# A bf16 copy of every second weight matrix, made once in HBM during the scan stage and read back by the MLP stages

## The reference, cut to what matters

```python
# layer 0, x is (4, 4096, 1024) f32
a = layernorm(x)
a2 = a + ssm_scan(rmsnorm(a, scale1), A, B, C, D)          # 16 states for each of 1024 channels
x = x + a2 + gelu(rmsnorm(a2, scale2) @ w1 + b1) @ w2 + b2  # w1 1024x4096, w2 4096x1024
u = layernorm(x)
x = x + u + sum over 2 shared experts of gelu(xn @ W1_s + b1_s) @ W2_s + b2_s
          + sum over the 2 chosen of 8 routed experts, weighted, of gelu(xn @ W1_r + b1_r) @ W2_r + b2_r
```

## Time and profile before

| what | us |
|---|---|
| median of 3 runs | 8356.27 |
| the runs | 8684.81, 8317.97, 8356.27 |
| the profiled execution | 8311.05 |
| its span, slowest core (core 2) | 8309.1 |
| spans of the 8 cores | 8291.6 to 8309.1 |
| PE busy, DVE busy, ACT busy, POOL busy | 5283.8, 2353.1, 1454.8, 1666.5 |

### The profile page before, as it was taken

One profiled execution on the slowest core, in us unless ns is written; L12 is line 12 of the kernel. 1 busy time (PEld: TensorE's weight loads), 2 busy tenths in 40 slices (PEclk: granted clock), 3 DMA queues, 4 the chain that ended last, 5 costly groups with the idle time before them and its releaser, 6 DMA issues.

```text
span 8309.1 us, 62744 instructions; the slowest of 8 cores (8291.6 to 8309.1 us)
## 1 busy us (share of the span) xinstructions
PE 5283.8 (64%) x22583; PEld 2288.5 (28%) x23040; DVE 2353.1 (28%) x2813; ACT 1454.8 (18%) x2046; POOL 1666.5 (20%) x1608
## 2 busy tenths in 40 slices
PE   0000000000787268889888898888888899888997
PEld 0000000000332123333333343333333334333333
DVE  5889898989112510000000000000000000000001
ACT  4760000000211021112111221112211122111220
POOL 0009696946000000001100111000110001001010
PEclk9855555555898689999999999999999999999997
DMA  3100000000453046666667666676666666666664
GB/s 92 23 0 0 5 0 5 0 5 3 62 84 56 15 76 99 104 102 91 99 104 106 91 96 92 102 106 87 96 92 103 100 95 92 95 102 102 91 92 105
DMA packets 555731, 597.23 MB, mean 72 GB/s; under 512 B 13194, under 2 KB 366362, under 8 KB 553764
## 3 DMA queue, kind: packets, MB, share of 16 engines
q0 software_dynamic: 545280, 566.28, 46.4%
q1 hardware_dynamic: 7844, 18.54, 0.7%
q10 hardware_dynamic: 2304, 8.39, 0.2%
HBM read 1134.22 MB, written 12.58 MB: 138 GB/s over the span
## 4 chain that ended last, share of the span: by engine, by line
PE 49%; DMA 19%; issue 14%; DVE 11%; POOL 5%; ACT 1%; DVEq 0%; POOLq 0%; ACTq 0%; SPq 0%
PE ps L873 23%; PE ps L907 18%; DMA WBUF<-W2r 11%; POOL SSb L266 4%; DMA STAT<-W1r 3%; PE ps L691 3%; DVE SSb L547 3%; DMA WBUF<-W2s 3%; PE ps L658 3%; DVE BIG L266 2%; DVE BIG L269 2%; DMA STAT<-W1s 1%; DVE MXS L269 1%; DVE MXS L266 1%; PE ps L957 1%
## 5 line engine op out<-in xcount | busy, mean ns | idle before, releaser
L907 PE MATMUL ps<-WBUF,XR 128*128 128x512 bf16 x10036 | 2361.5, 394 | 507.1 <-DMA WBUF<-W2r 288.2
L873 PE MATMUL ps<-MXS,STAT 128*128 128x512 bf16 x10034 | 2237.7, 382 | 158.4 <-DMA STAT<-W1r 61.5
L276 ACT ACTIVATE XR<-ps,BIA 128x512 bf16<-128x512 f32 x1280 | 879.4, 687 | 4214.6 <-PE ps L873 4214.4
L907 PEld LDWEIGHTS ps<-WBUF,XR 128*128 128x128 bf16 x10240 | 1014.7, 101 | 1853.9 <-issue 774.1
L873 PEld LDWEIGHTS ps<-MXS,STAT 128*128 128x128 bf16 x10240 | 994.6, 98 | 1401.3 <-issue 251.0
L269 DVE SCALAR_TENSOR_TENSOR BIG<-ps,WTOK,BIG 128x512 f32<-128x512 f32 x256 | 171.5, 742 | 4007.3 <-PE ps L907 4007.3
L419 PE MATMUL ps<-BIG,ONE 128*128 128x512 bf16 x32 | 14.3, 625 | 1432.0 <-ACT BIG L276 1432.0
L547 DVE TENSOR_TENSOR_SCAN SSb<-COEF,SSb,BIG 128x512 f32<-128x512 f32 x512 | 879.6, 1756 | 0.0
L280 POOL DMA_DIRECT2D WBUF<-W2r x256 | 190.0, 743 | 2102.2 <-PE ps L907 1892.1
L280 POOL DMA_DIRECT2D STAT<-W1r x256 | 224.2, 877 | 1657.1 <-PE ps L873 1514.7
L266 POOL TENSOR_TENSOR SSb<-SSb,COEF 128x512 f32<-128x512 f32 x256 | 472.4, 1845 | 164.0 <-DVE SSb L547 153.3
(11 more groups left out here) (82 smaller groups left out, 1464.1 us busy)
## 6 DMA issues: line engine op xcount, KB each, us to landing
WBUF<-W2r POOLq DMA_DIRECT2D x256, 1024.0 KB, 9.3
STAT<-W1r POOLq DMA_DIRECT2D x256, 512.0 KB, 6.0
WBUF<-W2s POOLq DMA_DIRECT2D x64, 1024.0 KB, 9.2
WBUF<-w POOLq DMA_DIRECT2D x32, 1024.0 KB, 9.7
STAT<-W1s POOLq DMA_DIRECT2D x64, 512.0 KB, 6.0
XR<-x SPq DMA_DIRECT2D x1, 8192.0 KB, 35.5
BIG<-xp SPq DMA_DIRECT2D x4, 2048.0 KB, 44.8
STAT<-w POOLq DMA_DIRECT2D x16, 512.0 KB, 11.2
```

What stands on the lines that cost most here:

```text
L276: return lambda e: e.activation(out, in0, fn, bias=bias, scale=scale, accum_out=acc)
L873: last = e.matmul(pp[:, 0:TT], w1c[:, dg * 256 + hs * 128: dg * 256 + (hs + 1) * 128], xn_bf[:, dg * TC + tq * TT: dg * TC + (tq + 1) * TT ...
L907: last = e.matmul(ps[tgl * 2 + dmh][:, 0:TT], hap[:, tgl * 128:(tgl + 1) * 128], w2t[:, dmh * 512:(dmh + 1) * 512], start=(hsub == 0), sto ...
```

## The change

A new tensor `w2c` in HBM holds a bf16 copy of all eleven W2 matrices, in the layout of a slot: 128 partitions, and for each of 88 quads 4096 elements (8 KB) in a row. Each core makes its own copy.

`w2cache_prep` makes the copy of one matrix. For each of its 8 quads, twice: SP loads half a quad in f32 (1 MB) into the first 2048 words of WBUF (the stage, which is slot 0), and ACT copies it as bf16 into one half of slot 1. Then SP stores slot 1 (1 MB) to `w2c`. There is one stage and one place for the result. The calls stand at the end of each tile `t` of P2: three matrices after tiles 0, 1 and 2, two after tile 3.

In P3 and P5 a quad's load becomes a plain copy of 1 MB bf16 from `w2c`, issued by SP. W1's loads stay on POOL as they are.

```diff
+    w2c_d = nc.dram_tensor("w2c", [128, (1 + NES + NER) * (HID // 512) * 4096],
+                           BF16, kind="Internal")
...
+        w2c_rg = [Rg(f"w2c{i}") for i in range(1 + NES + NER)]
...
+        def w2_quad_cols(m_idx, quad):
+            return (m_idx * (HID // 512) + quad) * 4096
+
+        def w2cache_prep(m_idx, src_ap_fn):
+            stage, st_rgs = w2slot[0]
+            stage_f32 = WBUF[:, 0:2048]
+            bld, bl_rgs = w2slot[1]
+            for quad in range(HID // 512):
+                for hq in range(2):
+                    b.dma("qs", DMA(
+                        stage_f32.rearrange("p (h2 d) -> p h2 d", d=D),
+                        src_ap_fn(quad * 512 + hq * 256)), writes=st_rgs)
+                    b.op("s", ACT(bld[:, hq * 2048:(hq + 1) * 2048],
+                                  stage_f32, AF.Copy),
+                         reads=st_rgs, writes=[bl_rgs[hq]])
+                c0 = w2_quad_cols(m_idx, quad)
+                b.dma("qs", DMA(w2c_d[:, c0:c0 + 4096], bld),
+                      reads=bl_rgs, writes=[w2c_rg[m_idx]])
...
             b.op("v", TTo(xt, xt, v3(y_ap, TT), ALU.add),
                  reads=xt_rgs + y_rgs, writes=xt_rgs)
+            nj = 3 if t < NT - 1 else len(prep_jobs)
+            for _ in range(min(nj, len(prep_jobs))):
+                mi, fn = prep_jobs.pop(0)
+                w2cache_prep(mi, fn)
...
                     if hsub % 4 == 0:
                         w2p, w2rgs = w2slot[psl]
-                        hrow = q * QH + hsub * 128
-                        b.dma("qg", DMA(
-                            w2p.rearrange("p (h2 d) -> p h2 d", d=D),
-                            dr["w2"][hrow:hrow + 512, :].rearrange(
-                                "(h2 p) d -> p h2 d", p=128)),
-                            writes=w2rgs)
+                        c0 = w2_quad_cols(0, q * 2 + hsub // 4)
+                        b.dma("qs", DMA(w2p, w2c_d[:, c0:c0 + 4096]),
+                              reads=[w2c_rg[0]], writes=w2rgs)
...
                 if hsub % 4 == 0:
                     w2p, w2rgs = w2slot[psl]
-                    b.dma("qg", DMA(
-                        w2p.rearrange("p (h2 d) -> p h2 d", d=D),
-                        w2_src2(hsub * 128)), writes=w2rgs)
+                    c0 = w2_quad_cols(w2m, hsub // 4)
+                    b.dma("qs", DMA(w2p, w2c_d[:, c0:c0 + 4096]),
+                          reads=[w2c_rg[w2m]], writes=w2rgs)
```

More of the change, by code:

```diff
@@ L431, in stats_sq_only @@
             return inv, ri
+        def w2_quad_cols(m_idx, quad):
[15 more added lines that the diff above has]
+                      reads=bl_rgs, writes=[w2c_rg[m_idx]])
+        w1slot = [(STAT[:, 0:1024].bitcast(BF16), [st_rg[0], st_rg[1]]),
+                  (STAT[:, 1024:2048].bitcast(BF16), [st_rg[2], st_rg[3]])]
+        w2slot = [(WBUF[:, 0:2048].bitcast(BF16), [wb_w2[0], wb_w2[1]]),
+                  (WBUF[:, 2048:4096].bitcast(BF16), [wb_w1[0], wb_w1[1]])]
         smid_ap = SSb[:, 4 * TT + GN:4 * TT + 2 * GN]
@@ L494, in build_program @@
                  reads=[smp_rg[pt], ss_smid], writes=[ss_smid])
+        prep_jobs = [(0, lambda hr: dr["w2"][hr:hr + 256, :]
+                      .rearrange("(h2 p) d -> p h2 d", p=128))]
+        for e_i in range(NES):
+            prep_jobs.append((1 + e_i, lambda hr, e_i=e_i:
+                              dr["W2s"][e_i, hr:hr + 256, :]
+                              .rearrange("(h2 p) d -> p h2 d", p=128)))
+        for e_i in range(NER):
+            prep_jobs.append((3 + e_i, lambda hr, e_i=e_i:
+                              dr["W2r"][e_i, hr:hr + 256, :]
+                              .rearrange("(h2 p) d -> p h2 d", p=128)))
         USO, YO, XBO = 0, G * TT, 2 * G * TT
@@ L623, in build_program @@
             return nc
[L625 to L628, removed]
         NQ = 4
@@ L851, in load_xn, with expert @@
                      reads=xn_all + [coef_rg], writes=xn_all)
-        def expert(eidx, w1_src, w2_src2, b1col, wcol):
+        def expert(eidx, w1_src, w2m, b1col, wcol):
             PSZ = min(2, n_slab5)
@@ L888, in expert, with mm2t_body @@
                 for tq in tqs:
-                    mm2t_body(tq, tq % n_slab5, w2_src2, wcol)
-        def mm2t_body(tq, slab, w2_src2, wcol):
+                    mm2t_body(tq, tq % n_slab5, w2m, wcol)
+        def mm2t_body(tq, slab, w2m, wcol):
             for hsub in range(NH):
@@ L935, in build_program @@
                    .rearrange("(dg p) h -> p dg h", p=128),
-                   lambda hr, e_i=e_i: dr["W2s"][e_i, hr:hr + 512, :]
-                   .rearrange("(h2 p) d -> p h2 d", p=128),
-                   NH + e_i * NH, None)
+                   1 + e_i, NH + e_i * NH, None)
         load_xn(4)
@@ L943, in build_program @@
                    .rearrange("(dg p) h -> p dg h", p=128),
-                   lambda hr, e_i=e_i: dr["W2r"][e_i, hr:hr + 512, :]
-                   .rearrange("(h2 p) d -> p h2 d", p=128),
-                   (1 + NES) * NH + e_i * NH, e_i)
+                   3 + e_i, (1 + NES) * NH + e_i * NH, e_i)
         for tg in range(NTG):
```

## The result

The changed kernel is slower: the ratio to the kernel before is 1.1095, with a 95% interval from 1.1035 to 1.1155. Its profiled execution took 9236.34 us, against 8311.05 before; the forecast was 9222.

The account below looks back on a forecast made before the run. It took P2 as bound by DVE and P5 by PE, whose waits were mostly for W2 loads. 8311 + 1443 (copies in P2) - 532 (P5: 362 + 40 + 130) = 9222 us, range 9000 to 9540.

Parts of the forecast that it names:

- The place of the price: P2's tile ends: casts stand between ACT's last pieces and next square, so ACT's 1383 idle us hide none of them.
- Its size: P2: 88 quads of 16.6 us in a serial chain, less 18 us, cost 1443 us (1311 to 1680).
- The sign that the forecast gave for the casts: P2: 176 casts of 1.96 us, each with some 4.6 us idle, ended by the DMA of W2 tiles.
- W2's waits in P5: P5: a reload takes 4.5 us, below the other slot's 6.9, so all 362 us of PE's waits go.
- The model holds: P5 before the change: 160 waits of 2.5 us give 400 us, against 362 measured; used for the changed loads.
- W1's waits: P5: with W2 loads off POOL, half of PE's 82 us waiting for W1 comes back, 40 us (0 to 82).
- The clock: P5: of 175 us lost to PE's low clock after waits, 130 come back (40 to 175).
- The sum: Whole kernel: 8311 + 1443 in P2 - 532 in P5 = 9222 us.
- Rival 2: P5: cached quads also come late, as widely spaced w2c rows read at half rate; 9590 us, 7 in 100.

Follow-up runs that it names:

- e9: Changed kernel with the copies' loads, casts and stores spread evenly over P2's 512 scans instead of the four seams; ratio to the kernel before 0.9379.
- e6: Changed kernel with the copies spread over P2's scans and two 512 KB stages in place of one; median 7751.7 us, ratio to the kernel before 0.9286.
- e2: Changed kernel without the stores of ten of the eleven copies, all experts using the first copy; 9009 us.
- e7: Changed kernel with each quad's reload from w2c in P5 done twice, one after the other; 9960 us on core 6.
- e4: Changed kernel with POOL instead of SP issuing the loads from w2c in P3 and P5; 9312 us.
- e8: Changed kernel with the rows of w2c 2 MiB apart in place of 704 KiB; 10251 us.

## Why the prediction was right, step by step

- **The place of the price.** "ACT's idle time hides none of them": shown. PE's and DVE's gaps at the first seam are 407 and 400 us, and e9 and e6 show the same casts all but free at another place in ACT's row.
- **Its size.** 1443 us forecast, 1437 measured. That these are so close is partly luck, as two errors in it nearly cancel. A load was put at 4.5 us and takes 5.0 with its semaphore steps in it, against the 4.7 of load and steps together; a store was put at 3.3 us ahead of the next load and costs 2.4 (e2). A quad comes to 16.4 us in place of 16.6. The cast was 1.91 us in place of 1.96. The sign that the forecast gave for the casts, some 4.6 us of idle time each, did not fit its own sum, since 16.6 us a quad leave 6.3 ahead of each cast; measured are 1101.3 / 176 = 6.3, as 5.0 and 7.6 in turn.
- **W2's waits in P5.** 362 us forecast to go, all but 3.5 went. The interpolated 4.5 us for a reload measured 4.8. "The model holds" said too much, though nothing hung on it: it counts 160 waits, where e7's timeline has fewer and longer ones, and it takes 0.1 us from PE's last matmul on a slot to the reload's issue, where the row below has 0.6 (the matmuls of the earlier trace rows that start at 3382.33 end at 3389.18). These errors go against each other, and at 4.8 us a reload is early by either way of counting.

```profile
3389.80 0.74 POOL L280 DMA_DIRECT2D WBUF<-W2s  x1 [7.89 <-PE ps L907]
```

- **W1's waits.** Half was forecast back, 40 us; it was 72 of 82. e4 shows why: 44 us (core 0) to 55 us (core 4) of them came from W1's loads standing behind W2's on POOL, more than the half that I had given to the seams between pairs. The 10 us that are left show that inside mm1 W1's loads are punctual enough.
- **The clock.** 130 us forecast. On core 0 the matmuls of P5 are busy for 4485 us, 61 over full speed; on core 3, the slowest, for 4550, 126 over it. So the waits gave back about 114 us on the one (175 - 61) and 49 on the other, where something new took 65. On the core that sets the time this is the term that was most mis-sized; the section below has it.
- **The sum.** P5 gave 5265 - 4758 = 507 us on the slowest cores, 532 forecast (busy and idle of both matmul groups, and above). Of these 359 are W2's waits, 72 W1's and 49 the clock; the other 27 are idle time with other causes, which the forecast did not have. 8311 + 1437 - 507 = 9241, measured 9236. On core 0 of the changed kernel P5 took 4699 us, 566 less than before, and the core ended at 9172. So the terms fit to some 30 us either way, and that the forecast came within 14 us of the slowest core is luck in part.
- **Rival 2** did not come, but the mechanism behind it is real at another spacing (e8). One reason for its 7 in 100 was that 704 KB is no power of two, and at that distance the loads were indeed early (4.8 us).

So the change wins 507 us in P5 on the slowest core, 566 on core 0, nearly all that its idea could give, and pays 1437 for it, because the copies stand at the ends of the tiles.

## What to carry to other kernels

An engine's idle time is of use only to instructions that stand before the thing it waits for: look at where new work falls in the row of its engine, not at how busy the engine is. The same loads, casts and stores cost 1437 us at the seams and about 60 between the scans; with a second stage as well nothing was left of the price, and 11% slower had become 7% faster. For a double-buffered load, compare its landing time with the work on the other slot: with 4.8 us against 6.9 the waits were gone, with 8.9 us and more they were there, very roughly the difference for each two loads, and each wait cost some of the clock as well. And look at the distance of the rows of a large HBM buffer: of the two tried, 704 KiB was harmless and 2 MiB was not.

## What the runs showed that was not expected

The distance of the rows in HBM: 4.8 us against 8.9 for the same load, 4.8 against 10.9 for the same store (e8).

The clock of a PE that no longer waits. Matmuls of P5 in windows of core 3 in the changed kernel, then the groups of core 0:

```profile
7233.37:7261.16 27.79, 27.79 (x128) 12.36 (x128) 4.46 (x7) 10.30 (x15) 2.62 (x3) 1.00 0.57 93
```
```profile
8106.12:8172.76 66.64, 66.64 (x256) 27.54 (x256) 0.00 (x0) 0.00 (x0) 0.00 (x0) 0.82 0.32 111
8173.83:8303.53 129.70, 129.70 (x512) 54.39 (x512) 4.47 (x7) 43.31 (x63) 13.11 (x15) 0.85 0.53 69
```
```profile
L942 PE MATMUL ps<-WBUF,XR 128*128 128x512 bf16 x10240 | 2253.5, 383 | 137.5 <-DVE BIG L272 111.4 <-ACT XR L279 20.5 <-DMA WBUF<-w2c 5.4
L908 PE MATMUL ps<-MXS,STAT 128*128 128x512 bf16 x10240 | 2231.8, 380 | 75.9 <-DVE MXS L265 37.3 <-DVE BIG L272 18.9 <-DMA STAT<-W1r 9.9
```

At full clock a matmul takes 27.79 / 128 = 0.217 us. From 8106 to 8304 us PE is busy without a gap but with a granted clock of 0.82 to 0.85, and 512 matmuls take 129.70 us, 0.253 each. Nothing in the program differs there from the pairs before and after it. This stretch costs core 3 some 30 us (768 matmuls at 0.217 are 167 us, they took 196); there is a second like it between 8800 and 9100 us. Cores 2 and 3 have them at the same times, and end at 9231 and 9235 us; the other six end at 9165 to 9177, and core 0 has a granted clock of 1.00 from 8106 to 8304. What sets them off was not tried.
